# A Mamba scan with a gated FFN: the softplus's subtraction moved to TensorE, SiLU of z from slot 63 to slot 60, the rows' low part from slot 19 to slot 21

## The reference, cut to what matters

```python
xz = hidden @ in_proj.T                      # 256 -> 1024; x, z = halves of 512 channels
u = silu(causal_conv_4_taps(x) + conv_b)     # per channel
x_dbl = u @ x_proj.T                         # 512 -> 64 + 16 + 16
delta = softplus(x_dbl[..., :64] @ dt_proj.T + dt_proj_b)      # 512 channels
h = exp(delta * A) * h + (delta * u) * B_t   # for each t: 512 channels x 16 states
y = sum_n(h * C_t) + u * D
x = layernorm(x + (y * silu(z)) @ out_proj.T)
f = silu(x @ w1.T * s1) * (x @ w2.T * s2)    # 256 -> 1024, ternary weights
f = gelu(f @ h1.T * sh1); f = gelu(f @ h2.T * sh2)             # 1024 -> 1024
out = layernorm(x + f @ w3.T * s3)
```

## Time and profile before

| | |
|---|---|
| median of 3 runs | 3012.06 us (3010.54 to 3012.91) |
| the profiled execution's own time | 3011.42 us |
| its span, first to last instruction | 3009.6 us |
| mean granted clock of TensorE | 0.953 of full speed |
| busy in the span: PE, DVE, ACT, POOL | 2720.0, 2297.7, 2033.7, 1704.2 us |
| the scans (L1284) | 1024 of 1268 ns, 1243.3 us |

### The profile page before, as it was taken

One profiled execution on the slowest core, in us unless ns is written; L12 is line 12 of the kernel. 1 busy time (PEld: TensorE's weight loads), 2 busy tenths in 40 slices (PEclk: granted clock), 3 DMA queues, 4 the chain that ended last, 5 costly groups with the idle time before them and its releaser, 6 DMA issues. The chain is left out here.

```text
span 3009.6 us, 40984 instructions
## 1 busy us (share of the span) xinstructions
PE 2720.0 (90%) x11540; PEld 1619.3 (54%) x11540; DVE 2297.7 (76%) x2650; ACT 2033.7 (68%) x3600; POOL 1704.2 (57%) x839
## 2 busy tenths in 40 slices
PE   5798998998998998998998976999999999999997
PEld 2243443343443443443443432778888888888886
DVE  6999999999999999999999999144445444444452
ACT  3878877878878877877878877465544555555452
POOL 4899999999899989999999998100000000000000
PEclk8899999998999999999999987999999999999999
DMA  8565565565566565565565566632222222222210
GB/s 265 122 188 158 144 190 158 144 193 164 134 193 165 136 192 159 139 196 158 139 192 165 143 186 224 205 101 77 92 70 70 84 91 77 70 79 88 70 42 15
DMA packets 239646, 412.05 MB, mean 137 GB/s; under 512 B 23264, under 2 KB 63456, under 8 KB 239456
## 3 DMA queue, kind: packets, MB, share of 16 engines
q1 hardware_dynamic: 175680, 297.67, 36.6%
q10 hardware_dynamic: 63776, 112.22, 11.4%
HBM read 285.55 MB, written 124.26 MB: 136 GB/s over the span
## 5 line engine op out<-in xcount | busy, mean ns | idle before, releaser
L1284 DVE TENSOR_TENSOR_SCAN h<-bank,state,db 128x512 f32<-128x512 f32 x1024 | 1243.3, 1268 | 18.9 <-ACT bank L916 18.5
L1144 POOL TENSOR_TENSOR hc<-h,c_rows 128x1024 f32<-128x1024 f32 x512 | 1200.3, 2375 | 96.6 <-DVE h L1284 75.0
L916 ACT ACTIVATE bank<-d_bc,a_neg 128x512 f32<-128x512 f32 x1024 | 695.4, 685 | 251.8 <-DVE h L1284 240.6
L1625 ACT ACTIVATE hring<-s_bank,sc 128x512 f32<-128x512 f32 x248 | 170.4, 687 | 488.6 <-PE s_bank L1558 488.3
L1558 PE MATMUL s_bank<-mid,h_r 128*128 128x512 f32 x2048 | 468.7, 390 | 4.6 <-DVEq L1652 4.6
L1268 DVE TENSOR_TENSOR db<-bank,du_bc 128x2048 f32<-128x2048 f32 x192 | 435.7, 2269 | 2.5 <-issue 2.5
L1558 PEld LDWEIGHTS s_bank<-mid,h_r 128*128 128x128 f32 x2048 | 385.5, 188 | 85.6 <-ACTq L1596 5.0
L731 PE MATMUL bank<-x_t,w 128*128 128x512 f32 x1088 | 362.5, 461 | 60.7 <-ACT ab L993 53.9
L659 PE MATMUL bank<-hc,fold_w 128*32 128x512 f32 x2048 | 305.1, 671 | 23.0 <-DVE uz L1308 11.3
L731 PEld LDWEIGHTS bank<-x_t,w 128*128 128x128 f32 x1088 | 203.2, 200 | 216.6 <-ACT ab L993 101.0
L1155 POOL TENSOR_TENSOR db<-du_bc,b_row 128x2048 f32<-128x2048 f32 x64 | 291.4, 4553 | 16.0 <-DVE h L1284 15.9
(11 more groups left out here) (147 smaller groups left out, 3721.7 us busy)
## 6 DMA issues: line engine op xcount, KB each, us to landing
ab<-ab ACTq DMA_DIRECT2D x272, 256.0 KB, 3.8
du_bc<-du_rows SPq DMA_DIRECT2D x256, 256.0 KB, 4.7
d_bc<-d_rows SPq DMA_DIRECT2D x256, 256.0 KB, 7.7
s_abr<-ab SPq DMA_DIRECT2D x120, 512.0 KB, 3.7
w<-w ACTq DMA_DIRECT2D x136, 256.0 KB, 3.1
d_rows<-sp_r SPq DMA_DIRECT2D x64, 256.0 KB, 2.0
du_rows<-sp_w SPq DMA_DIRECT2D x64, 256.0 KB, 3.1
x<-res SPq DMA_DIRECT2D x17, 512.0 KB, 8.8
```

Source lines behind the costliest of these rows:

```text
L916: act.activation(decays[DECAY_BANK[g]][:], d_bc[c % 2][:, j, :], ACT.Exp, scale=a_neg[:, g:g + 1]).then_inc(decay, 1)
L1144: pool.tensor_tensor(hc[:, k % HCSTEPS, at:at + HG], h[:, H_SLOT[k], at:at + HG], c_rows[:, q, :].unsqueeze(1).broadcast_to([P, HG, NT]), ...
L1284: dve.tensor_tensor_scan(h[:, H_SLOT[k], j, :], decays[DECAY_BANK[g]][:], db[:, k % DBSTEPS, j, :], state[:, g:g + 1], ALU.mult, ALU.add). ...
L1625: act.activation(hring[c % RING][:], p_h[m % HBANKS][:], ACT.Gelu, scale=sc[:, 2 + layer, m:m + 1]).then_inc(gelu, 1)
```

## The change

- **Softplus.** ACT writes the logarithm to a new SBUF buffer `sp_ln` instead of PSUM, and adds one activation that turns w into 1 - w. PE gets a new step 4, `logarithm_less`: two accumulating float32 matmuls with the identity put `ln(w) + (1 - w)` into `p_dt`. DVE loses its step 4; its step 5 becomes `min(p_dt, 0) + e`, and POOL adds instead of subtracting. DVE now waits for a new semaphore `sp_mm` of PE.
- **SiLU of z** moves from slot 63 to slot 60, the first slot of a step.
- **`low_rows`** moves on DVE from slot 19 to slot 21.
- **The ring** of `w1`/`w2` weights has three buffers instead of four, which makes room for `sp_ln`; the waits and the loads for the next tile are rewritten for three.

```diff
-SILU_Z_SLOT = 63
+SILU_Z_SLOT = 60
-ABRING, W12RING = 3, 4
+ABRING, W12RING = 3, 3
+        sp_ln = sb("sp_ln", [P, NT])
...
+            def logarithm_less(t, c):
+
+                pe.wait_ge(sp_act, t.count(5 * KI, 5 * c + 5))
+                pe.matmul(p_dt[:], w_id[:].bitcast(F32), sp_ln[:], start=True, stop=False)
+                pe.matmul(p_dt[:], w_id[:].bitcast(F32), sp_w[c % 2][:], start=False, stop=True).then_inc(sp_mm, 1)
...
                     for now, c in dt_places(t, i, 0):
                         if exists(now):
                             step_sizes(now, c)
+                    for now, c in dt_places(t, i, 4):
+                        if exists(now):
+                            logarithm_less(now, c)
...
-                    act.activation(x_ps[:], sp_e[:], ACT.Ln, bias=1.0).then_inc(sp_act, 1)
+                    act.activation(sp_ln[:], sp_e[:], ACT.Ln, bias=1.0).then_inc(sp_act, 1)
+
+                    act.wait_ge(sp_act, n + 3)
+                    act.activation(sp_w[k][:], sp_w[k][:], ACT.Identity, scale=-1.0, bias=1.0).then_inc(sp_act, 1)
...
-                    load_w12(t.following(), m - KH)
+                    load_w12(t.following(), e // 2 % W12RING)
...
-                    pool.tensor_tensor(sp_r[k][:], sp_r[k][:], sp_e[:], ALU.subtract).then_inc(delta, 1)
+                    pool.tensor_tensor(sp_r[k][:], sp_r[k][:], sp_e[:], ALU.add).then_inc(delta, 1)
...
-                if step == 4:
-                    dve.wait_ge(sp_act, t.count(4 * KI, 4 * c + 4))
-                    dve.scalar_tensor_tensor(out=p_dt[:], in0=sp_w[k][:], scalar=-1.0, in1=p_dt[:],
-                                             op0=ALU.add, op1=ALU.subtract).then_inc(sp_dve, 1)
-                elif step == 5:
-                    dve.wait_ge(sp_dve, t.count(2 * KI, 2 * c + 1))
-                    dve.scalar_tensor_tensor(out=sp_e[:], in0=p_dt[:], scalar=0.0, in1=sp_e[:],
-                                             op0=ALU.max, op1=ALU.subtract).then_inc(sp_dve, 1)
+            def softplus(t, c):
+                dve.wait_ge(sp_mm, t.count(KI, c + 1))
+                dve.scalar_tensor_tensor(out=sp_e[:], in0=p_dt[:], scalar=0.0, in1=sp_e[:],
+                                         op0=ALU.min, op1=ALU.add).then_inc(sp_dve, 2)
...
-                    if i == XD_SLOTS.stop + 1 and exists(nxt):
+                    if i == XD_SLOTS.stop + 3 and exists(nxt):
                         low_rows(nxt)
```

More of the change, by code:

```diff
@@ L305, in mamba_stage @@
         halo, silu_u, silu_z = sem("halo"), sem("silu_u"), sem("silu_z")
-        sp_act = sem("sp_act")
+        sp_act, sp_mm = sem("sp_act"), sem("sp_mm")
         sp_dve = sem("sp_dve")
@@ L712, in ffn_product @@
                 if which == 0:
-                    pe.wait_ge(w12_in[m % W12RING], t.count(16 * KH // W12RING, 16 * (m // W12RING + 1)))
+                    pe.wait_ge(w12_in[m % W12RING], t.count(16 * len(range(m % W12RING, KH, W12RING)), 16 * (m // W12RING + 1)))
                 before = product_before(t, e)
@@ L868, in softplus @@
                 k, x_ps = c % 2, p_dt
-                n = t.count(4 * KI, 4 * c)
+                n = t.count(5 * KI, 5 * c)
                 if step == 1:
@@ L1285, in scan @@
                                        state[:, g:g + 1], ALU.mult, ALU.add).then_inc(scanned, 1)
-            def softplus(t, c, step):
-                k = c % 2
-                if step == 4:
-                    dve.wait_ge(sp_act, t.count(4 * KI, 4 * c + 4))
-                    dve.scalar_tensor_tensor(out=p_dt[:], in0=sp_w[k][:], scalar=-1.0, in1=p_dt[:],
-                                             op0=ALU.add, op1=ALU.subtract).then_inc(sp_dve, 1)
-                elif step == 5:
-                    dve.wait_ge(sp_dve, t.count(2 * KI, 2 * c + 1))
-                    dve.scalar_tensor_tensor(out=sp_e[:], in0=p_dt[:], scalar=0.0, in1=sp_e[:],
-                                             op0=ALU.max, op1=ALU.subtract).then_inc(sp_dve, 1)
+            def softplus(t, c):
+                dve.wait_ge(sp_mm, t.count(KI, c + 1))
+                dve.scalar_tensor_tensor(out=sp_e[:], in0=p_dt[:], scalar=0.0, in1=sp_e[:],
+                                         op0=ALU.min, op1=ALU.add).then_inc(sp_dve, 2)
             def low_rows(t):
@@ L1364, in tile @@
                             times_b(now, g // JC)
[L1365 to L1368, removed]
-                    if i == XD_SLOTS.stop + 1 and exists(nxt):
+                    for now, c in dt_places(t, i, 5):
+                        if exists(now):
+                            softplus(now, c)
+                    if i == XD_SLOTS.stop + 3 and exists(nxt):
                         low_rows(nxt)
```

## The result

The changed kernel takes 3075.01 us (median of 4 runs, 3073.23 to 3078.45) against 3012.48 us for the kernel before: ratio 1.021, 95% interval 1.0193 to 1.0228, 62.5 us slower. The forecast was 3055 us, slower, with a range of 3018 to 3088. The profiled execution has a span of 3073.3 us, 63.7 more than before.

What follows compares the result with a forecast made beforehand. DVE, busy 97.7%, was taken to set the pace, with PE full for 47 us of every body. Terms of 10.5, 30.8 and 1.9 us gave +43 us on 3011.4, so 3055 us, range 3018 to 3088.

Steps and rivals of the forecast that it cites:

- the signs that were named: Profile signs of being right, among them about 115 us of DVE idle ahead of `min` and a 115.3 us period.
- c = 0, -1.1: First softplus chunk: DVE waits for nothing, saving 0.6 us, and `low_rows` in slot 21 saves 0.5 us a body.
- the cover that the forecast named: PE's idle time up to slot 37, 10.9 us a body, hiding its stand of about 1.4 us at the first chunk.
- c = 1, +1.8: Second softplus chunk: the new activation delays an ACT copy and PE, so DVE reads 1.8 us later, waiting some 2.6 us.
- Rival C: New products of one chunk run at half clock in each body: +1.8 us each, 27 us more, 3082 us; chance 0.14.
- c = 2, c = 3 and slot 1, +2.2 together: Stretch where PE is full: 1.5 us late at the third chunk, 2.2 us at the fourth, which includes it and slot 1's gain.
- SiLU of z at slot 60: ACT's SiLU moved earlier: the 1.2 us of DVE idle in slot 1 goes; a later convolution priced at 0, at most 0.8.
- two decays are made ahead: While the SiLU holds ACT 4.5 us, DVE has 3.4 us of scan and `db` work and two decays already prepared.
- The opening: Softplus before the first scan, with nothing to hide behind: +0.57 + 2.04 - 0.69 = +1.9 us.
- The ring of three: Three weight buffers instead of four: refills land in time, priced at 0, at most 3 us.
- the bounds of that range: 14 us for c = 0, the SiLU and the ring; 15 us the other way if PE absorbs 1 us more a body.
- Rival A: PE answers in time at all four chunks, DVE keeps its relief: 77 us faster, 2934 us; chance 0.13.

Runs made afterwards that it cites:

- "after": The changed kernel itself, with all parts of the change, against the kernel before: 3075.01 us, ratio 1.021.

## Why the prediction was right, and where its sizes were off

*The mechanism is shown.* From slot 48 to slot 10 PE is full, its products come late there, and DVE waits. Cutting PE's price from 1.72 to 0.70 us gave 47.6 us back, and taking other work out of PE ahead of c = 3 shortened that wait with the softplus untouched. Of the signs that were named, the idle ahead of the `min` line (133.9 us for about 115), the period (116.3 us for 115.3), c = 0 without a wait and the stretch without a pause came out. DVE's busy time fell by 35.6 us and not by 44: 44 is the 0.69 us of each L1291, of which only 0.60 us, 38.4 in all, were ever a slot's own, the rest being overlap with its neighbour.

*c = 0, -1.1.* Measured -1.05, with no wait for PE. PE's pause at slot 24 grew to 1.09 us from 0.30, its pauses at slots 28 and 29, 1.2 us, vanished, and that ahead of the product of slot 34 fell from 1.87 to 0.77: the cover that the forecast named. In the kernel with the earlier logarithm, `low_rows` alone was worth nothing that could be told. That its half of the -1.1 came true here may be luck: behind it stood a wait for PE that could swallow what it handed on.

*c = 1, +1.8.* This is the mis-sized term: +2.94. At full clock DVE waits 2.60 us, as forecast (2.6), and L639 starts behind the same ACT copy. But in 11 of 15 bodies the clock falls in slot 43; there the four records take 2.5 to 3.7 instead of 1.9 us, and the mean wait of all is 3.74. Rival C had this mechanism at this place, with 1.8 us a body and a chance of 0.14; the truth lies between: 1.1 us, 15 x 1.1 = 17 us, and another 1.8 us in the opening. The argument held against it, that PE is busier afterwards, looked at the wrong side. PE's pause before the rows' product is now 1.94 us, where the earlier trace rows show 0.66: 0.5 us of that is the copy, which the new activation delays, and 0.8 is PE, which gets to its FFN product 0.57 us behind the scan instead of 1.3. The filled pause shows that the clock stays full without this pause. It does not show that the pause alone decides: with the same pause, within 0.1 us, the clock stayed full in 3 of 14 bodies, and in the run with the softplus alone in 6 of 11; the one body of "after" with a shorter pause, 0.89 us, kept it too. What makes the difference between bodies stays open.

*c = 2, c = 3 and slot 1, +2.2 together.* Measured +1.9. The products take 1.72 and 1.81 us of PE's queue, where 1.8 was forecast; both pauses were absorbed as worked out; DVE waits 2.26 and 2.28 us instead of 2.5 and 2.7. (In the forecast's sum for c = 3 the convolution ends at 1477.64; the next product starts at 1477.73 in the earlier trace rows, a slip of 0.1 us.)

*SiLU of z at slot 60, priced by the idle of slot 1 alone.* Of the 1.2 us that were to go, 0.82 went, and the reason was wrong in part. The step "two decays are made ahead" held best where DVE stood still longest in slot 59: after the change (2.28 us) 0.24 us came back in slot 63, with one-pass products (1.06 us) 0.84, in the kernel before (none) 0.86. The fit is there; that the one causes the other is argued.

*The opening* cost 3.7 us instead of 1.9: the four records for c = 1 ran at the lower clock there and took 3.71 us, 1.8 more than at full clock. *The ring of three* was never run alone; no instruction of PE waits for one of its loads, and behind the scans the time is the same to 0.3 us.

*The sum.* Put in the forecast's own form, the measured terms give 15 x 1.9 + 14 x 1.9 + 3.7 = 59 us. The last scan ends 64.0 us later. The 5 us between lie mostly in slots that the form leaves out: the scans ahead of body 0 cost 2.4 us more than before, and body 15 with the closing scans 1.2. So 3075 us is the forecast's 43 us, some 19 us of half clock, and small terms of both signs; it stands at the upper edge of the range that the forecast gave itself, 3035 to 3075. The 14 and 15 us that were named as the bounds of that range do not add up to its 20 on either side, so the range was wider than the reasons given for it.

*Rival A*, the gain of 77 us, is refuted. The Trainium skill's rule to judge TensorE's headroom by the work done against the peak and the share of weight loads ("Perfetto Trace Analysis", Identifying the Most-Contended Engine) leads there: by the second of the two, 40% of the stretch after (555 of 1395 us), more than half of PE is free. The trace does not agree, since DVE waited 134 us for PE. Where the question is not the distance to the peak but whether an in-order queue can take 1.7 us more, the pauses in the timeline decide.

## What to carry to other kernels

Before moving work to an engine with a lower busy share, lay its timeline beside the slots and find where it has no pause: the same products cost nothing at c = 0 and made DVE wait 2.3 to 3.7 us at c = 1 to 3, and only a version that moved the free one alone was faster than the kernel before. Removing a wait on the engine that sets the pace can be worth nothing if another engine's queue has only the same few tenths of slack: four edits that each took 0.6 to 1 us a body out of the kernel before saw 0.25 us to nearly all of it return in other slots, and none made the kernel measurably faster. And when an added operation delays a release, count the pause it makes on the engine behind as well: here the clock of TensorE was halved behind such a pause in most bodies, just when the next thing it did was on the path.

## What the runs showed of the hardware

- In 11 of 15 bodies the granted clock fell from 2.4 to 1.2 GHz in slot 43, behind a pause of PE of 1.9 to 2.0 us, and four records then took 0.6 to 1.8 us more, 1.3 in the mean; in three bodies with the same pause it did not fall. With 1.7 us of useless products in the pause it stayed full in all 15, and the whole kernel was 9.5 us faster.
- Two float32 products of 128x512 take 1.72 to 1.92 us of PE's queue at full clock and 3.7 us at half; at full clock DVE starts 1.98 to 2.1 us after the first record starts. As one-pass products they take 0.70 us, 1.0 us less, which over 64 uses made the kernel 47.6 us faster, 0.74 us each.
